# A new second expert stage: units of two tiles, an inner layer made already turned, biases in the weight rows

## The reference, cut to what matters

```python
xf = layernorm(x).reshape(-1, 128)                 # 4096 tokens
scores = softmax(xf @ gate_w.T)                    # 8 experts
idx = top_k(scores + gate_b, 2)                    # two experts a token
rw[token, idx] = scores[token, idx]
h  = silu((xf @ w1[e] + b1[e]) * (xf @ w3[e] + b3[e]))   # inner width 176
y  = sum_e rw[:, e] * (h @ w2[e] + b2[e])
z  = the same with one shared expert (sw1, sb1, sw3, sb3, sw2, sb2) for every token
x  = x + y + z
```

## Time and profile before

| | us |
|---|---|
| median of 3 runs | 812.58 |
| lowest, highest | 806.71, 815.87 |
| span of the profiled execution | 806.3 |
| its own time, by the nearest run | 806.71 |
| PE, PEld, DVE, ACT, POOL busy | 756.4, 600.4, 511.8, 438.4, 502.1 |

### The profile page before, as it was taken

One profiled execution on the slowest core, in us unless ns is written; L12 is line 12 of the kernel. 1 busy time (PEld: TensorE's weight loads), 2 busy tenths in 40 slices (PEclk: granted clock), 3 DMA queues, 4 the chain that ended last, 5 costly groups with the idle time before them and its releaser, 6 DMA issues.

```text
span 806.3 us, 21917 instructions
## 1 busy us (share of the span) xinstructions
PE 756.4 (94%) x7293; PEld 600.4 (74%) x7293; DVE 511.8 (63%) x1602; ACT 438.4 (54%) x1137; POOL 502.1 (62%) x893
## 2 busy tenths in 40 slices
PE   6899999999998999999899999999987889998995
PEld 4677777776768999999767777777765667776773
DVE  2678888989752653444367799999985623333336
ACT  4456666665663434344146656665657556665662
POOL 7334577778774667666554457888776526766650
PEclk9899999999999999999979999999999999999998
DMA  8800000001022222222200101111212322222249
GB/s 233 361 2 2 9 27 24 22 32 33 29 83 73 72 75 67 75 71 58 79 27 21 38 28 58 45 58 39 58 47 79 96 52 81 80 82 74 75 112 281
DMA packets 65458, 57.63 MB, mean 71 GB/s; under 512 B 10596, under 2 KB 58724, under 8 KB 64807
## 3 DMA queue, kind: packets, MB, share of 16 engines
q1 hardware_dynamic: 56710, 38.27, 17.1%
q0 software_dynamic: 8640, 17.97, 6.6%
HBM read 34.03 MB, written 24.20 MB: 72 GB/s over the span
## 4 chain that ended last, share of the span: by engine, by line
PE 38%; POOL 25%; issue 14%; DVE 13%; DMA 3%; SPq 1%; ACT 1%; POOLq 1%; DVEq 0%
POOL results L1329 18%; PE ptp L1019 11%; PE M L1030 7%; PE S L1005 4%; PE S L1007 4%; POOL xi L1322 3%; PE M L1076 3%; DVE mx L822 2%; POOL rows L513 2%; DVE pr L823 2%; PE M L1079 2%; PE M L1038 1%; SPq L1299 1%; PE M L1047 1%; DMA first_w<-results 1%
## 5 line engine op out<-in xcount | busy, mean ns | idle before, releaser
L592 ACT ACTIVATE pT<-ptp 77x512 f32<-77x512 f32 x256 | 138.1, 588 | 142.3 <-PE ptp L1019 142.3
L1329 POOL DMA_INDIRECT results<-early,xi x142 | 149.2, 1051 | 90.7 <-DVE early L1401 87.9
L513 POOL DMA_INDIRECT rows<-out_rows,posi x128 | 127.1, 993 | 55.3 <-issue 25.5
L1019 PE MATMUL ptp<-cst,pr 128*77 128x128 f32 x1024 | 141.5, 282 | 0.2
L1345 ACT ACTIVATE early<-S 128x128 f32<-128x128 f32 x174 | 48.2, 277 | 152.0 <-PE S L1444 152.0
L1019 PEld LDWEIGHTS ptp<-cst,pr 128*77 128x77 f32 x1024 | 119.1, 150 | 13.5 <-ACT pT L592 8.4
L1393 DVE TENSOR_TENSOR hw<-hw,S 128x176 f32<-128x176 f32 x103 | 34.8, 337 | 108.1 <-ACT hw L1358 105.0
L822 DVE TENSOR_REDUCE mx<-S 128x16 f32<-128x1232 f32 x64 | 91.2, 1425 | 10.7 <-PE S L1007 10.0
L823 DVE TENSOR_TENSOR pr<-S,mx 128x1232 f32<-128x1232 f32 x64 | 92.3, 1442 | 2.2
L1451 PE MATMUL S<-W,early 128*128 (+1 forms) x206 | 79.8, 469 | 0.0
L1474 PE MATMUL ptp<-W,early 128*128 (+1 forms) x412 | 71.2, 296 | 7.7 <-DVE x_res L1408 7.5
(11 more groups left out here) (167 smaller groups left out, 1510.5 us busy)
## 6 DMA issues: line engine op xcount, KB each, us to landing
xs<-rows SPq DMA_DIRECT2D x142, 66.0 KB, 1.8
first_w<-in_e_W SPq DMA_DIRECT2D x2, 2048.0 KB, 10.5
swap<-results SPq DMA_DIRECT2D x32, 128.0 KB
first_w<-results SPq DMA_DIRECT2D x6, 512.0 KB, 7.5
results<-early,xi POOLq DMA_INDIRECT x142, 2.5
rows<-out_rows,posi POOLq DMA_INDIRECT x128, 2.3
rows<-out_rows SPq DMA_DIRECT2D x32, 64.0 KB, 1.6
xs<-rows SPq DMA_DIRECT2D x32, 64.0 KB, 2.0
```

The source lines that it names most:

```text
L513: nc.gpsimd.indirect_dma_start(rows[:, :], bass.IndirectOffsetOnAxis(posi[:, k, n:n + 1], 0), out_rows[:, ring_slot(groups, n), k, :], Non ...
L592: nc.scalar.activation(pT[:, r, :, :], ptp[r % 2][0:TK, :, :], ACT.Exp, scale=SCALE).then_inc(exp_done, 1)
L1019: last = nc.tensor.transpose(ptp[r % 2][0:TK, j, :], pr[:, n % 2, r * J + j, :], ident)
L1329: nc.gpsimd.indirect_dma_start(results[:, :], bass.IndirectOffsetOnAxis(xi[:, s:s + 1], 0), ys[:, s, :], None)\
```

## The change

`experts` now makes experts 0 only, and `gated_experts` replaces it for experts 1. Its work comes in units of two tiles: 14 units of shared batches, 36 units of routed tiles (the last has one tile), 2 units of shared batches.

```diff
-SHARED_FIRST = 20
+SHARED_FIRST = 28
-PACED = {(24, 1): 6, (25, 0): 7, (25, 1): 7, (26, 0): 8, (26, 1): 9, (27, 0): 10,
-         (28, 0): 12, (28, 1): 13, (29, 0): 14, (29, 1): 15, (30, 0): 16, (30, 1): 17}
+PACED = {(24, 1): 4, (25, 0): 5, (25, 1): 5, (26, 0): 6, (26, 1): 6, (27, 0): 7,
+         (28, 0): 8, (28, 1): 9, (29, 0): 10, (29, 1): 11, (30, 0): 12, (30, 1): 12}
...
+        def take(u):
+            for at, i in enumerate(tiles_of(u)):
+                in_place(pe, i)
+                last = nc.tensor.transpose(xTp(r)[:, at, :], xs[:, i % XU, 0:D], ident)
+        def widen(u):
+            wait(pe, hm_ready, 2 * u - 2)
...
+            if is_routed(u):
+                for at, _ in enumerate(tiles_of(u)):
+                    for c, out in enumerate(outs):
+                        last = nc.tensor.matmul(out[:, at * 128:(at + 1) * 128], w1s[:, u % 2, at, c * 128:(c + 1) * 128],
+                                                xsT[:, r % 3, at, :], start=True, stop=True)
+            else:
+                for c, out in enumerate(outs):
+                    last = nc.tensor.matmul(out, W1s[:, c * 128:(c + 1) * 128], xall[:, b * T:(b + 2) * T], start=True, stop=True)
+        def narrow(u, of):
...
+            for at in range(UNITS[u][2]):
+                for c in range(2):
+                    last = nc.tensor.matmul(yp(u)[:, at, :], hT[...], w2[:, c, :], start=(c == 0), stop=(c == 1))
+        for u in range(NU + 2):
+            if live(u):
+                widen(u)
+            yield u
+            if is_routed(u + 2):
+                take(u + 2)
+            if live(u - 2):
+                narrow(u - 2, of.pop(u - 2, None))
+            yield u
```

```diff
+        def w1_copies(u):
+            for at, i in enumerate(tiles_of(u)):
+                V.tensor_copy(w1s[:, u % 2, at, :], W1r[:, bass.ds(e, 1), :]...).then_inc(w1_copied, 1)
+        note(0)
+        for i in range(SLOTS):
+            if i % 2 == 0 and i + 2 < SLOTS:
+                note(i // 2 + 1)
+            send(i)
```

**Shared rows.** ACT's copy of the turned rows in attention 1 is split in two; the second goes to `xall`, which keeps the turned rows of all 32 batches on the chip:

```diff
+                if first < end:
+                    nc.scalar.activation(turned[:, first:end], M1[:, first:end], ACT.Copy).then_inc(turned_copied, 1)
+                if more:
+                    nc.scalar.activation(st["xall"][...], M1[:, 2 * T:(2 + len(more)) * T], ACT.Copy).then_inc(rows_turned, 1)
```

More of the change, by code:

```diff
@@ L33 @@
 N = B * T
[L34 removed]
 NBP = 128
[L36 removed]
+NB = 2 * D
 SLOTS = 2 * N // 128 + E - 1
@@ L1284, in turned @@
-    def turned(eng, n):
-        eng.wait_ge(xsT_ready, n + 1)
+        wait(sp, xi_copied, n - U + 1)
+        wait(sp, ys_ready, n - U + 1)
+        r = row_of(sp, n) if row is None else row
+        sp.dma_start(xs[:, s, :], rows[bass.ds(r, 128), :]).then_inc(xs_in[s], 16)
     def results_stored(sp):
         for s in range(U):
-            sp.wait_ge(ys_out[s], 16 * len([m for m in range(FIRST, FIRST + SLOTS) if m % U == s]))
+            sp.wait_ge(ys_out[s], 16 * len([m for m in range(SLOTS) if m % U == s]))
@@ L1368, in scalar, with x_copy @@
-        for n in range(NS + (2 if two else 0)):
-            if live(n + 2):
-                x_copy(n + 2)
-            if two and live(n - 2):
-                h_copy(n - 2)
-            if two and live(n):
-                up_copy(n)
-            if two and live(n - 1):
-                silu(n - 1)
-            if not two and live(n):
-                silu(n)
-            yield n
+        act.wait_ge(st["ones_set"], 1)
+        def x_copy(u):
+            r = u - ROUTED_AT
+            size = UNITS[u][2]
+            act.wait_ge(xsT_ready, r + 1)
+            nc.scalar.activation(xsT[:, r % 3, 0:size, :], xTp(r)[:, 0:size, :], ACT.Copy).then_inc(xsT_copied, 1)
@@ L1418, in add_results @@
             V.tensor_tensor(xb, xb, yg[:, 1, b0:b0 + HU, :], ALU.add).then_inc(x_done, 1)
-        late = 3 if two else 1
-        if not two:
-            dve.wait_ge(st["weights_in"], st["n_weights"])
-            w1_copy(0)
-        for n in range(NS + late):
-            if two and live(n):
-                hidden(n)
-            if not two and live(n + 1):
-                w1_copy(n + 1)
-            if live(n - late):
-                y_copy(n - late)
-            for half in range(len(ADDS_AT)):
-                if two and n == ADDS_AT[half]:
-                    add_results(half)
-            yield n
+        dve.wait_ge(st["w1_less"], E)
@@ L1436, in tensor @@
+        for u in range(NU + 2):
+            if is_routed(u + 1):
+                w1_copies(u + 1)
+            if live(u):
+                hidden(u)
+            yield u
+            if live(u - 2):
+                results_of(u - 2)
+            yield u
+        dve.wait_ge(z_ready, pairs_through(NU - 1))
+        for half in range(B // HU):
+            add_results(half)
     def tensor(pe):
         pe.wait_ge(st["weights_in"], st["n_weights"])
-        pe.wait_ge(st["bias_in"], 16)
-        def take(n):
-            pe.wait_ge(xs_in[n % U], 16 * (n // U) + 16)
-            wait(pe, xsT_copied, n)
-            nc.tensor.transpose(xTp, xs[:, n % U, 0:D], ident).then_inc(xsT_ready, 1)
@@ L1446, in widen @@
-        def widen(n, e):
-            pe.wait_ge(xsT_copied, n + 1)
-            if two:
-                wait(pe, hb_ready, n - 1)
-                nc.tensor.matmul(up[n % 2][:, 0:UW], xsT[:, n % 3, :], of_expert(W1, e), start=True, stop=False)
-                nc.tensor.matmul(up[n % 2][:, 0:UW], three[:, :], of_expert(w["B1"], e), start=False, stop=True).then_inc(up_ready, 1)
-                return
-            pe.wait_ge(w1_copied, n + 1)
-            for c in range(FC):
-                last = nc.tensor.matmul(hTp[n % 2][:, c, :], w1s[:, n % 2, c * 128:(c + 1) * 128], xsT[:, n % 3, :],
-                                        start=True, stop=True)
-            last.then_inc(hT_ready, 1)
```

578 lines of the change are left out of this document (358 added, 220 removed).

## The result

The changed kernel takes 792.33 us (median of four, 790.3 to 793.14) against 810.8 for the kernel before in the same comparison (806.71 to 815.87): a ratio of 0.9762, 95% interval 0.9726 to 0.9799. The forecast was 800 us, 12.6 us under the median known then (812.58); the medians of this comparison differ by 18.5 us.

What follows compares the result with a forecast made beforehand. PE bounds the routed stage before, POOL after the change: first send 663.9, plus 35 units of 2.95 gives 767.2, plus 25.4 and 1.5 gives a 794.1 us span; with 0.4 and 5.9 added, 800 us, range 786 to 813.

Steps and rivals of the forecast that it cites:

- PE's arithmetic: Routed stage: PE needs 1.23 us a tile against 1.64, saving 29 us if nothing else held the pace.
- Rows and first send: Before the routed stage: sorted rows there at 650.2 us, then 13.7 us to the first send at 663.9.
- the release of scatters by units: Attention's tail: scatters wait for shared units, last scatter 2 us later than before, bounds -2 and +5.
- Units: Routed stage: POOL's two sends and one note cost 2.80 us, with weight copies 2.95 us a unit, 35 times.
- the overlap with copies: Routed stage: DVE's weight copies mostly touch one of a unit's two sends, adding 0.14 us a unit.
- The rival of the full lock: Routed stage: POOL stands still for both weight copies, 3.52 us a unit, 20 us more, 820 us; chance 0.13.
- PE as the bound at 2.45: Routed stage: PE, not POOL, sets the unit at 2.45 us, 17.5 us less, 783 us; chance 0.08.
- The tail after the last send: Results land, are loaded back, added and stored: 25.4 us, 0.7 saved as no shared tile sits behind.
- Setup, experts 0 and attention 1: Stages ahead: setup 0, experts 0 +0.5 us from late loads, attention 1 +1 us from ACT's split copy.
- the sign the prediction had named: Attention 1: an iteration 0.07 us longer, as ACT's copy becomes two instructions.
- Span and median: Whole kernel: execution time 0.4 us above its span, median 5.9 above that, so 794.1 gives 800 us.
- The rival of the clock: Routed stage: PE stays at the lower clock, 4.9 us a unit, 68 us more, 868 us; chance 0.04.

Runs made afterwards that it cites:

- condition B: Three of the four sets of runs (chips numbered 9, 12 and 14), in which the kernel before took 827 to 830 us as median.
- condition A: The first comparison and the fourth set of runs (chip numbered 9 again), in which the kernel before took 810.8 and 809.85 us.
- the kernel with stretches: Changed kernel with sends, loads or both left out for stretches of routed tiles, against the kernel before: 788.97 us against 809.85, ratio 0.9743.

## Why the prediction was right, and where not

The mechanism was right: POOL becomes the bound, the 29 us of PE's arithmetic can't be had in full, and the start of the stage slips. The profiled execution was forecast with a span of 794.1 us and has 790.7. Two larger errors of opposite sign stand behind that small difference: the first send 7.0 us too early, the units together 9.3 us too long. With 0.4 us in the tail and 1.5 us of additions that net to nothing (below), they make the 3.4. That the span came so near is luck in part; which engine bounds the stage is not.

**Rows and first send: 663.9 forecast, 670.88 measured, 7.0 too early.** The last scatter was put 2 us later than before and came 7.3 later (651.20 against 643.86). The term that failed is the release of scatters by units. By the text's own sum unit 12 is through at 644 and the last scatter starts at 648, 4 us later than before; it then took 2, with no reason but the bounds. And unit 12 was later than that: its products end at 647.12, and the last scatter that waits for a unit starts at 647.40. Two of these 3 us are the last ranks, which came 1 us sooner (626.01 against 627.05) and not 3. The rest is PE's clock. The unit behind the ranks and the next one took 3.2 and 2.9 us where later ones take 2.19; the granted clock is 0.90 from 620 to 640 us, where before had 1.00, and already from 610 to 620 it is 0.50 to 0.53 where before had 0.77 to 0.89. POOL stood 9.82 us before the first such scatter and 0.67 to 2.71 before four others. The bounds of this term were -2 and +5; it lay outside. A further 0.9 us came in the way of rows (5.3 from the last scatter to the first note, before 4.3). PE stood 8.47 us, not 6, and began its units cold, as forecast: eight passes in 2.05 us at 657.19 where 1.05 is the rate at the full clock. The ramp from there to the first send was 14.4 instead of 13.7.

That the waits for units are the cause has an experiment only in condition B: without them the last scatter started at 663.83 and the first send at 689.15, against 678.27 and 697.54 for the changed kernel in the next set. That is 8.4 us for the first send, and much the size of the error. But the two runs are of different sets, and the same code ahead of the stage moved by up to 10 us between kernels of that condition (last scatter 671.53 to 682.17), so I call it supported and not shown. The size in condition A was not measured.

**Units: 2.95 us forecast, 2.69 measured, 35 units 9.3 us shorter.** Two sizes were off. The first is the gap between note and send: 0.31 was taken from rows 5, where a send waits for DVE (the row says so), and it is 0.16 where the sender waits for its own note. That makes the base 2.64 and not 2.80, 5.6 us over the stage. The lesson is in the brackets of the row: a gap with a releaser is the releaser's. The second is the overlap with copies. 0.14 us a unit was taken, about 0.05 is the mean (2.69 less 2.64). Ten sends take over 1.00 us, up to 1.17. Each of them starts while a copy runs that has 0.19 us or more to go, as in experts 0 (703.32 above, over whose start the copies of 702.77 run); five that start in the last 0.12 us of a copy are no longer than others. A copy that begins inside a send costs the send nothing. That is so for 25 of the 71 sends, and it is the case that the prediction's rival feared:

```profile
742.34 0.96 POOL L1541 DMA_INDIRECT results<-early,xi  x1 [0.30 <-DVE early L1614]
742.41 0.36 DVE L1595 COPY w1s<-W1r 128x384 f32 x1
...
743.01 0.45 DVE L1595 COPY w1s<-W1r 128x384 f32 x1 [0.24 <-issue]
```

The first of these copies lies wholly within the send, and neither takes longer than alone. The second begins late in the send, takes 0.45 and ends 0.16 us after it, and so do all 15 copies of over 0.40 us: they end 0.15 to 0.17 us after a send does. The rival of the full lock (3.52 us a unit) is out. That copies can be held up shows in their durations. Twelve copies in the stretch without sends, and those of the changed kernel with sends:

```profile
L1606 DVE COPY w1s<-W1r x12: 359/360/361, 699.8 to 712.5; 128x384 f32 x12
```
```profile
L1595 DVE COPY w1s<-W1r x68: 340/360/599, 663.9 to 748.6; 128x384 f32 x68
```

So each engine can wait for the other for part of an instruction: a send by up to 0.18 us (1.17 against 0.99), a copy by up to 0.24, on the mean 0.03 (0.39 against 0.36). The Trainium skill (SBUF — State Buffer, "SBUF: two separate sides") has an exclusive lock for the whole instruction of DVE; these rows agree that POOL and DVE get in each other's way, and not that either stands still for the whole of the other's instruction, since the copy of 742.41 and the send around it run at once at full speed.

**PE as the bound at 2.45 (0.08).** Out, but near: the stage is 94.0 us and would be 87.5, as the kernel with stretches shows. The forecast had put the distance at 17.5 us, as it held POOL for slower than it is.

**The tail after the last send:** 25.4 forecast, 25.8 measured.

**Setup, experts 0 and attention 1.** 0, +0.5 and +1 forecast. POOL's rows from 595 to 602 us stand within 0.1 us of each other in both kernels, but two effects cancel there. The changed kernel is 2.2 us ahead by 40 us, and still 2.0 at the last send of experts 0 (386.17 against 388.18). This lead is hardly work saved: between 25 and 35 us the granted clock was 0.68 and 0.64 in the trace of before and 1.00 in this one, and in the kernel with stretches, whose code is the same there, it was 0.66 again from 30 to 35. So it looks like the execution's and not the change's. Experts 0 costs 0.1. Attention 1 then loses the lead. PE's products behind ACT's copies come 6.26 us after those of the iteration before (504.50 after 498.24), where the kernel before has 6.13 (505.19 after 499.06). From 435 to 560 us PE's weight loads wait 6.8 us for the copies in 20 iterations instead of 4.4, so 0.12 each. That is the sign the prediction had named, with 0.07: the split copy costs nearly twice what was taken, 2.4 us in these 20 iterations, and at 595 us the lead of 2.0 is gone.

**Span and median.** 0.4 and 5.9 us were added to the span, since the execution nearest to the profile of before was its quickest (806.71). The 0.4 is wrong: in all 59 executions with both figures on record the time is 1.8 to 2.1 us above the span, so the span of 806.3 belongs to about 808.1 us, and that lies 4.5 under the median. In the changed kernel the median is 1.6 us above the span of the profile. So of the 7.7 us between forecast and result, 3.4 are the span and the rest is this step, which carries the spread of one kernel to another. The lower end of the range is a slip as well: its terms add up to about 12 us, which gives 788 and not 786; the result lies above both.

**The slower side.** The rival of the clock (0.04) didn't come in condition A: 1.00 through the stage. In condition B the changed kernel is slower than before. The clock does fall there in the stage (0.91 in two of the three windows above), but behind PE's idle time (after the 2.16 us of 708.12 its next eight passes take 2.07 us instead of 1.06) and for a part of a window, not through the stage as that rival had it; the units of 3.7 us come from the late starts behind PE. No rival of the forecast names this, and the profile of before had no row that could have told. What could have been said is the form of the risk: in the new stage POOL is within 0.2 us of PE's cycle of 2.45 and DVE, busy 16.7 of 20 us, within 0.4, where the old one has PE far above the rest. That this form is what made the new stage slow in condition B is not shown, since the old stage met no late starts there.

## What to carry to other kernels

When PE gets faster, add up the next engine's cycle from gaps whose releaser is that engine itself; a gap that ended on another engine is no cost of it. Work that waits for units by a written order must be priced again when units change in size, with the clock that PE will have there, and it can eat two fifths of a gain. A copy beside a send is priced by where it lies: here only one that ran over the send's start cost the send anything. And a gain of 2% should be timed on more than one chip and at more than one time: this one is a loss of 2.9% in the other condition, in a stage where handoffs came over 3 us late, while the old stage took the same time in both.

## What the runs showed beyond that

In condition B ACT starts 0.04 us after the products it waits for in the first four units, as in A, and then up to 3.4 us after them. The onset is the same in all ten traces of the changed kernel and its variants in this condition. SP's register moves take up to 0.72 us instead of 0.04, and the kernel before shows neither in its routed stage. Sends and loads of an eighth of the rows change nothing in that. Two additional notes make the stage 10.7 us shorter. The cause wasn't found, and the one kernel that leaves out whole transfers met condition A. No version was found that beats both kernels in both conditions: in A the changed kernel is ahead by 2.4%, in B the kernel before by 2.9%, and the nearest there is the changed kernel with two useless notes, 1.3% behind.
